# Four rows instead of two side by side in a cross-shaped channel mixing kernel on one Trainium2 core

## The reference, cut to what matters

```
wI = w + eye(16)
ret = einsum('BGMTS,GMN->BGNTS', x, wI)
hq = einsum('BGMTS,BTGIM->BGITS', x, qw1);  ret += einsum('BGITS,BTGIM->BGMTS', hq, qw2)
hk = einsum('BGMTS,BSGIM->BGITS', x, kw1);  ret += einsum('BGITS,BSGIM->BGMTS', hk, kw2)
ret += x * qdd[t] + x * kdd[s]
```

## Time and profile before

| | |
|---|---|
| median of 3 runs | 859.1 us (857.77 to 862.08) |
| the profiled execution: its time, its span | 858.88 us, 857.1 us |
| PE matmul busy | 766.5 us (89%) |
| DVE, ACT, POOL busy | 546.1 (64%), 393.6 (46%), 513.6 us (60%) |
| mean granted TensorE clock | 0.976 of full |
| moved by DMA | 157.09 MB, mean 183 GB/s |

### The profile page before, as it was taken

The page is one execution under the profiler, slowest core; times in us unless marked ns, Lnnn a source line. Parts: engine busy times, 40 slices in busy tenths (PEclk is TensorE's granted clock), DMA queues, the critical chain, the costliest instruction groups (busy, mean ns, idle before and its releaser), DMA issues.

```text
span 857.1 us, 42054 instructions
## 1 busy us (share of the span) xinstructions
PE 766.5 (89%) x18464; PEld 704.4 (82%) x18464; DVE 546.1 (64%) x809; ACT 393.6 (46%) x673; POOL 513.6 (60%) x456
## 2 busy tenths in 40 slices
PE   5998899799898999797998899979998889988998
PEld 2658799699787988797987898868998779877997
DVE  3338557468474866665676675837758566665668
ACT  6224563247432583225833466325743267324640
POOL 2326577467665677555766567646776567765733
PEclk9999999999999999989999999999999999999999
DMA  9804318952568618774098723785167840985026
GB/s 190 296 3 100 93 59 309 295 185 66 200 213 296 180 25 293 232 282 101 3 333 237 265 75 131 277 277 183 44 245 257 297 110 6 341 251 184 4 116 278
DMA packets 76045, 157.09 MB, mean 183 GB/s; under 512 B 39768, under 2 KB 40792, under 8 KB 73944
## 3 DMA queue, kind: packets, MB, share of 16 engines
q1 hardware_dynamic: 75888, 154.61, 55.5%
HBM read 85.25 MB, written 69.34 MB: 180 GB/s over the span
## 4 chain that ended last, share of the span: by engine, by line
POOL 34%; PE 25%; issue 24%; DVE 7%; DMA 5%; SPq 2%; POOLq 1%; ACT 1%; DVEq 0%; ACTq 0%
POOL WA L200 19%; POOL WB L208 9%; PE PB L655 7%; PE PA L607 7%; POOL WB L200 6%; PE PA L642 5%; PE PB L624 4%; DMA X<-in_x_dram 3%; DVE OUT L524 3%; PE PB L592 3%; DVE WB L208 2%; SPq L240 1%; DVE PROD L478 1%; DMA RT<-products 1%; DVE PROD L481 1%
## 5 line engine op out<-in xcount | busy, mean ns | idle before, releaser
L524 DVE TENSOR_TENSOR OUT<-PB,X 128x512 f32<-128x512 f32 x256 | 172.4, 686 | 185.0 <-PE PB L655 141.0
L402 ACT ACTIVATE Y<-PA 128x512 f32<-128x512 f32 (+1 forms) x256 | 147.3, 634 | 306.7 <-PE PA L607 306.7
L412 ACT ACTIVATE X<-PA 64x512 f32 (+3 forms) x384 | 232.7, 606 | 118.5 <-PE PA L642 111.8
L655 PE MATMUL PB<-Y,WB 128*128 128x128 f32 x2048 | 272.6, 286 | 1.7 <-issue 1.0
L655 PEld LDWEIGHTS PB<-Y,WB 128*128 128x128 f32 x2048 | 248.8, 193 | 15.8 <-issue 6.2
L208 POOL TENSOR_TENSOR WB<-RT,mask 128x512 f32<-128x512 f32 x128 | 156.3, 1221 | 106.1 <-PE PB L655 102.6
L511 DVE TENSOR_TENSOR Y<-PB,Y 128x512 f32 (+1 forms) x256 | 164.8, 685 | 80.7 <-PE PB L624 69.5
L607 PEld LDWEIGHTS PA<-X,WA 64*64 64x64 f32 x8192 | 149.4, 145 | 78.1 <-issue 37.8
L642 PE MATMUL PA<-Y,WA 64*64 64x128 f32 x4096 | 190.9, 311 | 20.7 <-issue 14.3
L607 PE MATMUL PA<-X,WA 64*64 64x64 f32 x8192 | 170.1, 234 | 44.0 <-DMA X<-in_x_dram 25.3
L200 POOL TENSOR_TENSOR WA<-RS,mask 128x512 f32<-128x512 f32 x128 | 139.4, 1089 | 110.7 <-PE PA L642 85.4
(11 more groups left out here) (24 smaller groups left out, 62.4 us busy)
## 6 DMA issues: line engine op xcount, KB each, us to landing
X<-in_x_dram SPq DMA_DIRECT2D x128, 512.0 KB, 6.0
out_dram<-OUT SPq DMA_DIRECT2D x128, 512.0 KB, 4.5
RT<-products SPq DMA_DIRECT2D x15, 1024.0 KB
products<-PROD SPq DMA_DIRECT2D x16, 128.0 KB, 8.2
RT<-products SPq DMA_DIRECT2D x1, 768.0 KB
QP<-in_rows_dram SPq DMA_DIRECT2D x8, 80.0 KB, 3.5
RT<-in_left_dram SPq DMA_DIRECT2D x1, 384.0 KB
RT<-products SPq DMA_DIRECT2D x1, 256.0 KB
```

Of the source, the lines that this page charges most:

```text
L402: nc.scalar.activation(rows_of(Y, k, j)[:, :, WIDE * h:WIDE * (h + 1), :].rearrange("q a s c -> q a c s"), PA[HALVES * (j % RING) + h][:, ...
L412: nc.scalar.activation(columns_of(block_of(X, k), dst, WIDE * i + NARROW * g), by_columns(PA[HALVES * (g % RING) + i][src, :]), ACT.Copy). ...
L524: nc.vector.tensor_tensor(rows(OUT[:, o % OUT_SLOTS]), PB[g % SLOTS][:, :].rearrange("q (a c s) -> q a c s", a=FEW2, c=PAIR), rows(rows_of ...
L655: last = nc.tensor.matmul(PB[g % SLOTS][:, COLS * r:COLS * (r + 1)], WB[:, g % SLOTS, P * r:P * (r + 1)], rows_of(Y, k, t2_chunk(o))[:, (i ...
```

## The change

`PAIR` goes from 2 to 4. All shapes follow from it: `PAIRS` (64 to 32), `CHUNK2` (4 to 2), `FEW2` (2 to 1). The buffers keep their size, every instruction and every transfer its count and its number of elements, and the order, the waits and the matrices stay. What differs is how the same values lie: those of one row now stand 16 bytes apart, and those of a column in pieces of four rows, 16 bytes, with 2,048 bytes from piece to piece.

```
-PAIR = 2
+PAIR = 4
 PAIRS = ROWS // PAIR
```

## The result

The changed kernel takes 1,092.95 us (median of 4 runs, 1,091.92 to 1,097.31) against 860.59 us of the kernel before on the same chip: a ratio of 1.271, 95% interval 1.265 to 1.277. It is 27% slower. Forecast were 1,105 us, range 890 to 1,185. The profiled execution took 1,091.92 us, with a span of 1,090.1.

What follows compares the result with a forecast made beforehand. PE, busy for 89% of the span, was taken to bound the kernel. From 858.9 us, +304 (PE along rows), -28 (PE along columns) and -30 (stalls) gave 1,105 us, range 890 to 1,185.

Steps and rivals of the forecast that it cites:

- A: PE pays the full price along rows, 1.7 ns a column: 1,105 us, own range 1,000 to 1,185; chance 0.64.
- step 1: PE's reads along rows in t1 and t2, values 16 bytes apart: 1.7 ns a column instead of 0.9, +304 us.
- the stalls: In T, longer rounds let X's transfers come in time, so waits and some half-speed time go: -30 us.
- B: PE pays less, 1.0 to 1.4 ns a column, if memory gives a line every 1.06 ns: 966 us; chance 0.16.
- Step 2: PE's reads along columns in s1 and s2, pieces of 16 bytes instead of 8: -28 us, between 20 and 37.
- Step 3: DVE's and ACT's accesses along rows (lines 524, 402): adds 0.27 to 0.46 us longer, covered by PE, cost nothing.
- rival D: PE keeps up, S gains nothing or DVE's longer adds take it back, 3 us a block: 850 to 870; chance 0.08.
- Step 4: DVE's and ACT's accesses along columns (lines 511, 412): price already that of values side by side, no change.
- At half clock nothing is lost: PE at half clock already takes about 1.7 ns a column, so the start (70 us) stays as it is.

Runs made afterwards that it cites:

- experiment 1: Kernel before (PAIR 2) with only PE's moving operands of t1 and t2 stepping 16 bytes instead of 8: 1,119.9 us, ratio 1.296.
- experiment 2: Changed kernel (PAIR 4) with only PE's moving operands of t1 and t2 stepping 8 bytes: 866.7 us, ratio 1.004.
- experiments 10 to 12: Changed kernel, halved: ACT's copies (line 412); these and DVE's adds (line 511); GpSimd's matrices for odd s1 groups alone: 1,084.3, 1,085.6, 1,088.0 us.
- experiment 3: As experiment 2, with DVE's adds of line 524 also reading X and writing OUT at 8 bytes: 839.3 us, ratio 0.965.

## Why the prediction was right

The time came out 12 us under the forecast, by the mechanism given, and A was the case that happened. That it came so near is partly luck: step 1 cost 25 to 29 us more than forecast and the stalls gave back some 31 us more, two errors of opposite sign that cancel. Term by term:

- *Step 1, PE along rows: forecast +304, measured 2,048 x 0.112 + 1,792 x 0.058 = 229 + 104 = +333 us.* The cause is shown by experiment 1 and its reverse, experiment 2. The price of 1.7 ns a column was 1.75; of its two sources, DVE's scattered read (1.6) was short and the halving of PE's own pace (1.8) a little long. Counted by stretches it is nearly the same: 112 rounds of T at 5.81 us instead of 3.11 are 302 us, and the last stretch adds 27. B's idea, a memory pace of one line in 1.06 ns shared by the quarters, is refuted: `t1` with four quarters pays per column what `t2` pays (58 ns for 64, 112 for 128).
- *Step 2, PE along columns: -28, measured -32.6 for the S stretches as a whole.* The size was right by two errors that cancel. I held 19 ns a round, the distance to a `t2` pass, for all that could be won. PE won 33 to 36: the floor of a `t2` pass isn't the floor of a quarter round. And I named DVE's 4.0 us in two steps as what would hold S; halving DVE's and ACT's work there moved it by 7.5 us at most, and PE's own stops took more (experiments 10 to 12).
- *Step 3, DVE and ACT along rows: nothing while PE covers them.* DVE's adds cost 0.76 ns more an element (0.53 to 0.9 forecast), T has it busy for 47.0 us (44 to 50 forecast). With the cover taken away it cost what rival D said, some 3 us a block (experiment 2), and experiment 3 put it on DVE. One part was never covered: at the turn into S, where up to 7 us were forecast for DVE and left out of the sum, DVE waited 11 us longer for ACT's copies and PE 8 us longer for DVE. It is inside the -32.6.
- *Step 4: nothing.* Lines 511 and 412 kept their price.
- *Stalls: -30, measured about -61* (what the 241.4 us of the seven T stretches leave beside 302). Here the size was off by half. All seven T stretches take 92.7 us, exactly 16 rounds of 5.8; the 25.3 us of waits for X are 1.4, the 14.3 us of idle time ahead of line 607 put down to issue are 0.2, and the granted clock over these stretches went from 0.97 to 1.00. I had kept half of T's stalls, and none was left. With the start's -3.0 the terms close: 302 + 27 - 61 - 33 - 3 = 233 up to rounding.
- *At half clock nothing is lost:* nearly. In the start 64 records of `t1` took 1.92 us before, the half clock's pace, although the row of that stretch gives 1.00. In the changed kernel they took 2.05 us between 30 and 40 us, where the granted clock was 0.50, and 2.00 us between 50 and 60 us, where it was 1.00. So at half clock the price is 7%, and the start didn't grow for the reason that step 1 gives. That it fell from 70.0 to 67.0 us is another matter: PE ran at the faster pace in its second half (1.06 us for a pair of line 592 instead of 2.00), and the layout doesn't explain that.

What the Trainium skill says ("Advanced Engine Details and Errata", SBUF Cachelines: two hits on a 16-byte line are needed, another line for each access is penalised) holds for PE's float32 operand at 2.4 GHz. The two-hit boundary agrees with the runs: 4 and 8 bytes cost nearly the same (124 and 126 ns a pass), 16 bytes nearly double a column. No run has a step between 8 and 16 bytes.

## What to carry to other kernels

When a layout serves reads in two directions, write down how many values each direction finds in 16 bytes: the direction that falls from two to one loses about as much as it costs already, while the direction that goes from two to four gains a quarter here, and only part of that arrives. Price a step that the trace doesn't show on one engine from a scattered operation on another, and check which distance, not only which piece size, a column has: a gap of 16 bytes behind 1,024 gave 1.9% for a little unused memory. A change that loses on the bounding engine may hide a second loss on a covered one; here, mending PE's reads alone brought the kernel only back to where it was.

## What the runs showed of the hardware that I had not expected

- A value alone costs PE 1.75 ns at 16 bytes from the next, 1.8 at 32 and 2.15 at 512, the last in the quarters of `s1` and `s2`; whether the distance does it or its being a power of two is open. Pieces of 8 bytes cost 145 ns a round at 1,024 bytes, 122 at 1,032 and 117 at 1,040.
- A round of four quarters along 16-byte pieces, 109 ns for 128 columns, beats a full-array pass over values side by side, 124 ns.
- PE stops in the middle of groups that no semaphore guards, in S 26 times for 34.7 us in the changed kernel and 11 times for 19.6 in the slower groups of before. They keep step with the loads of instructions; no run tested it.
